# Perceiver block on one core: part of the probability transposes through DMAs, the second context through ScalarE, and a new order of the value products

## The chip, the cores and the metric

The kernel runs on 1 core of one Trainium2 chip. The metric is the device time of one execution in microseconds (us); before the change it is 512.61 us, the median of 3 runs (512.58 to 512.73).

## The reference, cut to what matters

`x` is two batches of 128 tokens by 512 features; the context is two batches of 2048 tokens by 512. The kernel computes three residual blocks; the change lies in the first.

```
k = split_heads(ctx @ Wk + bk); v = split_heads(ctx @ Wv + bv)   # 16 heads of 32
q = split_heads(layernorm(x) @ Wq + bq)
attn = softmax(q k^T / sqrt(32), over the 2048 context tokens)
x = x + (attn @ v) @ Wo + bo
x = x + self_attention(layernorm(x)) with its own layer norm, gamma, beta
x = x + FFN of 4 experts, one chosen per token (argmax), GELU, layer norm
```

All is float32. Products whose operands are split into a rounded part H and a rest L (type fp32r) are made as three matmuls (H*H, L*H, H*L).

## The kernel before, in words

The cross attention works in 8 steps `p` (NP = 8): batch `p // 4`, group `p % 4` of 4 heads (HPG = 4, G = 4). The 2048 context tokens lie in 4 chunks `c` of 512 (C = 4). There is no loop over steps that is shared by the engines: each engine has its own program, a queue that runs in order, and they meet at semaphores. In each program stands the loop `for p in range(1, NP + 1)` (L1502 TensorE, L571 ScalarE, L1032 VectorE); its turn `p` is called **pass p** here. Pass p makes the keys and the scores of step p, and turns the probabilities of step p-1 and multiplies them with the values.

What pass p holds, by function:

- `keys(p, c)`, TensorE (through `product`, L1158): 12 matmuls of 512 columns into PSUM bank 6 (bank 3 for c = 1). ScalarE then writes the rounded part `KrH` (L440), VectorE the rest `KrL` (L735). Both have KR = 3 slots, indexed by c.
- `scores(p, c)`, TensorE (L1212): 12 matmuls into banks 0 to 3, one bank per head, in three rounds of four heads. The first round of a chunk waits, head by head, until VectorE has read the chunk before (`s_done`).
- `negative_scores(p, c)`, VectorE (L755): per head, negates the scores into `Pm`, with the running minimum. It waits for the transpose of the same chunk and head of step p-1, which frees that place of `Pm`.
- `exponentials(p-1, i)`, ScalarE (L454): the exponential of head i over all 2048 tokens, in place in `Pm`.
- `probs_T(p-1, c, i)`: TensorE transposes four 128x128 blocks (L1228) of chunk c and head i into bank 4 or 5; ScalarE copies them into `PT` (L462), which has two slots (c % 2). I call one such unit a **turn**; a pass has 16.
- `weighted_values(p-1, c)`, TensorE (L1242): 32 matmuls with `V`, called WV(c) below. It ends the use of a slot of `PT` (`pv_mm`).
- `reciprocals_T` (L1250), `outputs`: the denominators. ScalarE copies the transposed reciprocals to `RT` (L470) between its second and third exponential.

The order of TensorE in pass p, written out by hand: keys 0, WV(3) of step p-2, `reciprocals_T`, keys 1, turns 0-0 and 0-1, keys 2, turns 0-2 and 0-3, scores 0, then for c = 1: two turns, WV(0), two turns, scores 1, keys 3; for c = 2: two turns, WV(1), two turns, scores 2; for c = 3: two turns, WV(2), two turns, scores 3. ScalarE: exp 0, KrH 0, exp 1, RT, exp 2, KrH 1, copies 0-0 and 0-1, exp 3, KrH 2, copies, and so on.

Some passes carry more. After pass 4 (p = G) come the 16 value products of batch 1 (`while_values`) with the self attention of batch 0 among them, which I call **the value stretch**. Passes 5 to 7 carry the rest of the self attention and the router of batch 0 (`alongside` on VectorE; `attention2_out` in pass 6; `normalized_T`, `logits` and `masks` in pass 7). Pass 8 has no keys and no scores, but the first expert matmuls (`first_experts`, L1423).

The context of batch 1 is loaded in passes 3 and 4: SyncE issues the four loads `raw` (L287) when the keys of pass 3 have read the chunk, and GpSimd makes `ctxH` (L400) and `ctxL` (L402) of each. GpSimd has nothing else to do in the passes, but for some `rsqrt` of one column (L385).

## Time and profile before

| | |
|---|---|
| median of 3 runs | 512.61 us |
| the profiled execution, its own time | 511.96 us |
| its span in the trace | 510.2 us |
| TensorE matmul busy | 494.2 us (97%) |
| VectorE busy | 304.8 us (60%) |
| ScalarE busy | 264.4 us (52%) |
| GpSimd busy | 42.2 us (8%) |
| TensorE clock granted | 9 or more tenths of full speed in all slices but the last (8 tenths) |

The profile is of one execution. Busy shares say little of where time can be won; the order of events within one pass says more, and this is read from the timeline (instructions of one engine in order) and from the chain that ended last. In those, "idle before" is the time that an engine stood still ahead of an instruction, with the instruction that released it.

### The profile page before, as it was taken

What the parts mean: (1) busy time and instruction counts of PE and PEld (TensorE: products, weight loads), DVE (VectorE), ACT (ScalarE), POOL (GpSimd) and SP (SyncE); (2) the same over time, 40 slices, a digit from 0 to 9 for tenths busy, and PEclk for the clock granted to TensorE, in tenths of its full rate; (3) what the DMA queues carried; (4) which work ended last, traced back from release to release, by engine and by line L of the source; (5) the groups of instructions that cost most, each with busy time, mean ns of one, the idle gap of its engine ahead of it and who ended that gap; (6) DMA issues with size and microseconds to landing.
All of it is one profiled execution on the core that took longest, in us unless ns stands there. A gap on an engine that the chain in (4) does not pass through costs nothing.

```text
span 510.2 us, 9250 instructions
## 1 busy us (share of the span) xinstructions
PE 494.2 (97%) x3742; PEld 377.6 (74%) x3742; DVE 304.8 (60%) x584; ACT 264.4 (52%) x400; POOL 42.2 (8%) x34
## 2 busy tenths in 40 slices
PE   8999998999999999999999999999999999999995
PEld 5786777777777777898877778766686867877663
DVE  3747542645565553246178376669379988965962
ACT  4230027485767632327347748567436756654730
POOL 0030000000099000000000000000002010000000
PEclk9999999999999999999999999999999999999998
DMA  8900000000341012220210000099377898875001
GB/s 279 360 1 1 1 1 0 2 1 1 94 162 79 1 45 109 96 84 0 82 65 3 0 1 1 10 418 397 107 284 294 302 387 362 297 288 240 1 0 41
DMA packets 11353, 62.47 MB, mean 122 GB/s; under 512 B 1584, under 2 KB 2096, under 8 KB 4528
## 3 DMA queue, kind: packets, MB, share of 16 engines
q1 hardware_dynamic: 11024, 61.62, 31.8%
q8 instruction: 30, 0.49, 0.4%
q10 hardware_dynamic: 288, 0.27, 0.2%
q14 instruction: 11, 0.09, 0.0%
HBM read 61.36 MB, written 0.52 MB: 121 GB/s over the span
## 4 chain that ended last, share of the span: by engine, by line
PE 84%; ACT 7%; issue 3%; DVE 2%; DMA 1%; SPq 0%; POOLq 0%; POOL 0%; ACTq 0%; DVEq 0%
PE ps L1158 36%; PE ps L1228 11%; PE ps L1242 6%; PE ps L1212 5%; ACT Pm L454 4%; PE ps L1479 3%; PE ps L1480 3%; PE ps L1481 3%; PE ps L1423 3%; PE ps L1499 3%; PE ps L1433 2%; PE ps L1435 2%; PE ps L1434 2%; DMA wv_raw<-in_xWv 1%; PE ps L1152 1%
## 5 line engine op out<-in xcount | busy, mean ns | idle before, releaser
L755 DVE TENSOR_SCALAR_CACHE_REDUCE Pm<-ps,small 128x512 f32<-128x512 f32 x96 | 66.4, 748 | 30.5 <-PE ps L1212 30.4
L462 ACT COPY PT<-ps 128x512 f32<-128x512 f32 x128 | 68.4, 591 | 29.0 <-PE ps L1228 29.0
L1228 PE MATMUL ps<-ident,Pm 128*128 128x128 f32 x512 | 69.3, 277 | 3.1 <-ACT Pm L454 3.1
L1228 PEld LDWEIGHTS ps<-ident,Pm 128*128 128x128 f32 x512 | 56.5, 141 | 18.0 <-issue 10.9
L454 ACT ACTIVATE Pm<-Pm,small 128x2048 f32<-128x2048 f32 x32 | 64.3, 2011 | 3.5 <-DVE Pm L755 3.5
L735 DVE SCALAR_TENSOR_TENSOR KrL<-ps,small,KrH 128x512 fp32r<-128x512 f32 x32 | 23.9, 747 | 61.2 <-ACT KrH L440 61.2
L1158 PE MATMUL ps<-wvH,ctxH 128*128 128x512 f32 x124 | 50.3, 406 | 1.0 <-DVE V L744 1.0
L1158 PE MATMUL ps<-ctxH,wkH 128*128 128x512 f32 x124 | 51.1, 412 | 0.0
L1158 PE MATMUL ps<-ctxL,wkH 128*128 128x512 f32 x124 | 48.6, 392 | 0.0
L1158 PE MATMUL ps<-ctxH,wkL 128*128 128x512 f32 x124 | 48.5, 391 | 0.0
L1158 PE MATMUL ps<-wvH,ctxL 128*128 128x512 f32 x124 | 48.4, 390 | 0.0
L1158 PE MATMUL ps<-wvL,ctxH 128*128 128x512 f32 x124 | 48.4, 390 | 0.0
L440 ACT ACTIVATE KrH<-ps,small 128x512 fp32r<-128x512 f32 x32 | 22.0, 688 | 47.2 <-PE ps L1158 46.6
L1124 DVE TENSOR_TENSOR w2L<-w2raw,w2H 128x2048 fp32r<-128x2048 f32 x15 | 34.2, 2289 | 10.7 <-ACT w2H L651 10.7
L651 ACT CAST w2H<-w2raw 128x2048 fp32r<-128x2048 f32 x15 | 28.7, 1911 | 19.0 <-PE ps L1481 18.5
L1242 PE MATMUL ps<-PT,V 128*32 128x128 f32 x1024 | 34.6, 276 | 1.0 <-ACT PT L462 1.0
L449 ACT COPY V<-ps 128x512 f32<-128x512 f32 x16 | 9.3, 584 | 47.8 <-PE ps L1158 45.3
L385 POOL TENSOR_TENSOR small<-small 128x1 f32<-128x1 f32 x10 | 6.8, 678 | 326.9 <-DVE small L716 326.9
L1242 PEld LDWEIGHTS ps<-PT,V 128*32 128x32 f32 x1024 | 26.0, 109 | 8.2 <-issue 6.0
L1158 PEld LDWEIGHTS ps<-ctxH,wkH 128*128 128x128 f32 x124 | 23.5, 190 | 9.3 <-issue 5.0
L1158 PEld LDWEIGHTS ps<-wvH,ctxH 128*128 128x128 f32 x124 | 23.3, 188 | 8.0 <-issue 2.0
L744 DVE COPY V<-ps 128x512 f32<-128x512 f32 x16 | 11.0, 689 | 29.3 <-PE ps L1158 29.3
(235 smaller groups left out, 869.9 us busy)
## 6 DMA issues: line engine op xcount, KB each, us to landing
w1raw<-in_W SPq DMA_DIRECT2D x16, 1024.0 KB, 6.1
w2raw<-in_W SPq DMA_DIRECT2D x15, 1024.0 KB, 4.9
raw<-in_ctxT SPq DMA_DIRECT2D x7, 1024.0 KB, 4.8
woF<-in_ffn_Wo SPq DMA_DIRECT2D x4, 1024.0 KB, 9.9
wo<-in_wo SPq DMA_DIRECT2D x2, 1024.0 KB, 4.9
ctx_first<-in_ctxT SPq DMA_DIRECT2D x4, 256.0 KB, 4.6
wv_raw<-in_xWv SPq DMA_DIRECT2D x2, 512.0 KB, 8.0
wq<-in_xWq SPq DMA_DIRECT2D x1, 1024.0 KB, 13.0
```

Source lines behind the costliest of these rows:

```text
L440: act.activation(KrH[:, c % KR, :], ps[:, bank, :], ACT.Identity, bias=bias3[:, 1, p % G:p % G + 1], scale=1.0).then_inc(k_hi, 1)
L454: act.activation(Pm[:, i, :], Pm[:, i, :], ACT.Exp, bias=mx[:, p % 2, i, C - 1:C], scale=-1.0, accum_out=den[:, p, i:i + 1]).then_inc(exp_ ...
L462: act.copy(PT[:, c % 2, i, :, :].rearrange("p k t -> p (k t)"), ps[:, t_bank(p, c, i), :]).then_inc(pt_done, 1)
L651: act.copy(w2H[n % 3][:], w2raw[n % RING2][:]).then_inc(w1_hi, 1)
L735: dve.scalar_tensor_tensor(KrL[:, c % KR, :], ps[:, bank, :], bias3[:, 1, p % G:p % G + 1], KrH[:, c % KR, :].bitcast(F32), ALU.add, ALU.s ...
L755: dve.tensor_scalar(Pm[:, i, c * CH:(c + 1) * CH], ps[:, i, :], -1.0, mx[:, p % 2, i, c - 1:c] if c else NOT_YET, ALU.mult, ALU.min, accum ...
L1124: dve.tensor_tensor(w2L[n % RING2][:], w2raw[n % RING2][:], w2H[n % 3][:].bitcast(F32), ALU.subtract).then_inc(w1_split, 1)
L1158: mm = pe.matmul(dst, l, r, start=(n == 0), stop=(n == len(pairs) - 1))
L1212: last = pe.matmul(ps[:, i, :], l[q, g, b * T:(b + 1) * T], r[q, c % KR, :], start=(k == 0), stop=(k == len(terms) - 1))
L1228: last = pe.transpose(ps[:, t_bank(p, c, i), j * P:(j + 1) * P], Pm[:, i, c * CH + j * P:c * CH + (j + 1) * P], ident[:])
L1242: last = pe.matmul(ps[q, PV_BANK, 0:T], V[:, c * JT + j, (HPG * g + i) * DH:(HPG * g + i + 1) * DH], PT[:, c % 2, i, j, :], start=(c == 0 ...
L1423: last = pe.matmul(ps[:, c, :], zt, w1raw[RAW_OF[t]][:, c * CH:(c + 1) * CH], start=(t == 0), stop=False)
```

## The change

1. For steps 0 to 6 (`by_dma`), heads 0 to 2 (HD = 3) of chunks 2 and 3 (PEC = 2) are no longer turned by TensorE. GpSimd copies the 512 words of each into `stage` as two planes of 512 half words (`probs_split`), SyncE issues a `dma_start_transpose` of 128 x 1024 half words (256 KB) from `stage` back into `Pm` (`turned`), and GpSimd weaves the planes together into `PT` (`probs_merged`). `stage` holds one head of each of the two chunks, so the copy of the next head waits for the DMA of the last. A turn remains for head 3 of these chunks: 10 of 16 turns in a pass stay with TensorE. Step 7 is turned as before.
2. `negative_scores(p, c)` of these heads waits for `merged[c]` instead of the transpose; WV(2) and WV(3) wait for `merged[c]` too.
3. KR is 2 instead of 3 (the room goes to `stage`): `KrH` of chunk c waits for the scores of chunk c-2. ScalarE makes it for chunk 2 behind the copies 0-2 and 0-3; VectorE makes `KrL` of chunks 2 and 3 behind the negations of chunks 0 and 1.
4. The loads of batch 1's context are issued by ScalarE, `ctxH` is made by ScalarE (`context_high`), `ctxL` by VectorE (`context_low`), in passes 3 and 4.
5. TensorE's order: WV(2) moves to the next pass, before WV(3); WV(0) and WV(1) stay among the turns and scores; keys 3 comes behind WV(1); the first 8 of the 12 matmuls of the next pass's keys 0 (EARLY) come before scores 3, but not in passes 3, 4 and 7 (`early_keys`). After pass 4, the first value product comes before WV(2) and WV(3).
6. The transposed outputs of batch 0's self attention (`outputs2_T`, pass 5) are all copied by ScalarE instead of half by VectorE. Some one-time semaphores are merged, and two `rsqrt` of GpSimd stand between its new copies.

The diff, cut to its core:

```diff
-        KR = 3
+        KR = 2
+        stage = at("stage", [P, 2, 2, CH], U16, 184)
...
+        def by_dma(p, c, i):
+            return p < NP - 1 and c >= PEC and i < HD
...
+        PEC = C // 2
+        HD = HPG - 1
...
@@ sync
-            for c in range(C):
-                sp.wait_ge(k_mm, C * (G - 1) + c + 1)
-                sp.dma_start(raw[c][:], a["ctxT"][C + c]).then_inc(raw_in[c], 16)
+            def turned(p, i):
+                for c in range(PEC, C):
+                    sp.wait_ge(p_split, 2 * (HD * p + i) + c - PEC + 1)
+                    sp.dma_start_transpose(Pm[:, i, c * CH:(c + 1) * CH].bitcast(U16).rearrange("p (k t) -> p k t", t=T),
+                                           stage[:, c - PEC, :, :].rearrange("p h n -> p (h n)")).then_inc(p_turned[c], 16)
...
@@ gpsimd
+            def probs_split(p, i):
+                pool.wait_ge(exp_done, HPG * p + i + 1)
+                for c in range(PEC, C):
+                    if HD * p + i:
+                        pool.wait_ge(p_turned[c], 16 * (HD * p + i))
+                    words = halves_of(Pm[:, i, c * CH:(c + 1) * CH])
+                    pool.tensor_copy(stage[:, c - PEC, :, :], words.rearrange("p n h -> p h n")).then_inc(p_split, 1)
+            def probs_merged(p, c, i):
+                pool.wait_ge(p_turned[c], 16 * (HD * p + i + 1))
+                if i == 0:
+                    pool.wait_ge(pv_mm, slot_user(p, c))
+                words = halves_of(PT[:, c % 2, i, :, :].rearrange("p k t -> p (k t)"))
+                halves = Pm[:, i, c * CH:(c + 1) * CH].bitcast(U16).rearrange("p (h n) -> p h n", h=2)
+                pool.tensor_copy(words.rearrange("p n h -> p h n"), halves).then_inc(merged[c], 1)
+            for p in range(NP - 1):
+                probs_split(p, 0)
+                probs_split(p, 1)
+                if p == G + 1:
+                    rsqrt(LN3[0])
+                probs_split(p, 2)
+                for i in range(HD):
+                    probs_merged(p, PEC, i)
+                if p == G + 1:
+                    rsqrt(LN4[0])
+                for i in range(HD):
+                    probs_merged(p, PEC + 1, i)
...
@@ scalar, keys(p, c)
-                    act.wait_ge(s_mm, (n if c == C - 1 else p * C) * HPG - (2 * HPG if c == C - 1 else 0))
+                    act.wait_ge(s_mm, (n - KR + 1) * HPG)
...
+            def context_in(c):
+                act.wait_ge(k_mm, C * (G - 1) + c + 1)
+                act.dma_start(raw[c][:], a["ctxT"][C + c]).then_inc(raw_in[c], 16)
+            def context_high(c):
+                act.wait_ge(raw_in[c], 32 if c else 16)
+                act.copy(ctxH[c][:], raw[c][:]).then_inc(ctx_hi1, 1)
...
@@ vector, negative_scores(p, c)
-                    if p:
-                        dve.wait_ge(t_mm, n - C * HPG + 1)
+                    if p and by_dma(p - 1, c, i):
+                        dve.wait_ge(merged[c], HD * (p - 1) + i + 1)
+                    elif p:
+                        dve.wait_ge(t_mm, turned_before(p - 1, c, i) + 1)
...
+            def context_low(c):
+                dve.wait_ge(ctx_hi1, c + 1)
+                dve.tensor_tensor(ctxL[c][:], raw[c][:], ctxH[c][:].bitcast(F32), ALU.subtract).then_inc(ctx_split1, 1)
...
@@ vector, the passes
                 for c in range(C):
                     if p < NP:
                         negative_scores(p, c)
-                        if c == 1:
-                            keys(p, 3)
+                        if p == G - 1 and c == 1:
+                            context_low(0)
+                        if c < 2:
+                            keys(p, c + 2)
+                        if p == G and c == 0:
+                            context_low(3)
+                        if p == G - 1 and c == 3:
+                            context_low(1)
...
@@ tensor, the passes
-                    keys(p, 0)
+                    keys(p, 0, (EARLY if early_keys(p) else 0, 3 * KT))
                 if late:
+                    weighted_values(p - 2, C - 2)
                     weighted_values(p - 2, C - 1)
                     reciprocals_T(p - 2)
...
+                    probs_T(p - 1, 1, 2)
+                    probs_T(p - 1, 1, 3)
+                    scores(p, 1)
+                    weighted_values(p - 1, 1)
+                    keys(p, 3)
+                    probs_T(p - 1, 2, 3)
+                    if p == G + 3:
                         masks(0)
+                    scores(p, 2)
+                    probs_T(p - 1, 3, 3)
+                    if early_keys(p + 1):
+                        keys(p + 1, 0, (0, EARLY))
+                    scores(p, 3)
                 if p == G:
+                    while_values(0)
+                    weighted_values(p - 1, C - 2)
                     weighted_values(p - 1, C - 1)
-                    while_values(0)
                     reciprocals_T(p - 1)
```

## Rows read from the trace of the kernel before

**Rows 1.** The page, part 1: busy us, share of the span, instructions.

```profile
PE 494.2 (97%) x3742; PEld 377.6 (74%) x3742; DVE 304.8 (60%) x584; ACT 264.4 (52%) x400; POOL 42.2 (8%) x34
```

**Rows 2.** The chain that ended last, 104 to 136 us: start, length, what.

```profile
104.16 2.96 PE ps L1158 x12
...
116.20 0.90 PE ps L1212 x11
117.10 1.02 PE ps L1228 x8
118.12 1.01 PE ps L1242 x32
...
121.06 2.95 PE ps L1158 x12
...
131.78 2.96 PE ps L1158 x12
```

**Rows 3.** Timeline of ScalarE, pass 3: start, length, instruction, idle before.

```profile
132.61 2.01 ACT L454 ACTIVATE Pm<-Pm,small 128x2048 f32<-128x2048 f32 x1 [0.59 <-DVE Pm L755]
...
135.34 2.00 ACT L454 ACTIVATE Pm<-Pm,small 128x2048 f32<-128x2048 f32 x1
...
140.99 2.03 ACT L454 ACTIVATE Pm<-Pm,small 128x2048 f32<-128x2048 f32 x1
```

**Rows 4.** Timeline of TensorE, pass 3: the turn that waits for the fourth exponential.

```profile
143.16 0.66 PE L1228 MATMUL ps<-ident,Pm 128*128 128x128 f32 x4 [0.36 <-ACT Pm L454]
```

**Rows 5.** Timeline of VectorE, end of pass 2 and pass 3.

```profile
127.84 0.75 DVE L755 TENSOR_SCALAR_CACHE_REDUCE Pm<-ps,small 128x512 f32<-128x512 f32 x1 [2.33 <-PE ps L1212]
...
130.53 0.18 DVE L764 RECIPROCAL small<-small 128x4 f32<-128x4 f32 x1
```

**Rows 6.** The page, part 5, and the groups by shape: GpSimd's and VectorE's context work.

```profile
L400 POOL CAST ctxH<-raw 128x2048 fp32r<-128x2048 f32 x4 | 7.6, 1900 | 108.6 <-DMA raw<-in_ctxT 108.6
L402 POOL TENSOR_TENSOR ctxL<-raw,ctxH 128x2048 fp32r<-128x2048 f32 x4 | 18.4, 4589 | 0.3
L728 DVE TENSOR_TENSOR ctxL<-raw,ctxH 128x2048 fp32r<-128x2048 f32 x3 | 6.9, 2291 | 0.1
```

**Rows 7.** DMA issues by line: count, KB each, median us from issue to landing.

```profile
rowsF<-in_rows SPq DMA_DIRECT2D x3, 256.0 KB, 8.6
b1raw<-in_b SPq DMA_DIRECT2D x1, 256.0 KB, 2.7
out_dram<-u SPq DMA_DIRECT2D x1, 256.0 KB, 2.0
```

**Rows 8.** Timeline of SyncE's queue: issue time of one DMA on an engine's queue.

```profile
188.45 0.33 SPq L290 DMA_DIRECT2D wS<-in_xWo  x1
```

**Rows 9.** The chain that ended last, at the borders of the other passes.

```profile
159.40 2.96 PE ps L1158 x12
...
252.95 5.67 PE ps L1158 x24
...
278.69 2.94 PE ps L1158 x12
...
309.21 2.95 PE ps L1158 x12
```

**Rows 10.** The same chain, passes 7 and 8.

```profile
329.84 0.70 ACT KrH L440
...
330.56 0.76 DVE KrL L735
...
339.92 3.67 PE ps L1423 x8
...
344.89 0.03 ACT RT L470
```

**Rows 11.** Timeline of VectorE, passes 5 and 6: the first instruction of each side job.

```profile
272.63 0.68 DVE L897 TENSOR_TENSOR u<-attnT,rows 128x512 f32<-128x512 f32 x1
...
296.98 0.75 DVE L908 SCALAR_TENSOR_TENSOR u<-u,small,rows 128x512 f32<-128x512 f32 x1
```

More of the change, by code:

```diff
@@ L13 @@
 F32R = mybir.dt.float32r
+U16 = mybir.dt.uint16
 ALU = mybir.AluOpType
@@ L240, in perceiver_block @@
         s_mm, s_done = sem("s_mm"), sem("s_done")
+        p_split = sem("p_split")
+        merged = {c: sem(f"merged{c}") for c in range(PEC, C)}
+        p_turned = {c: sem(f"p_turned{c}") for c in range(PEC, C)}
         exp_done, t_mm = sem("exp_done"), sem("t_mm")
@@ L314, in ffn_wo_in @@
                 sp.dma_start(woF[:, k, :], a["ffn_Wo"][:, k, :]).then_inc(woF_in, 16)
+            for p in range(G + 1, NP - 1):
+                for i in range(HD):
+                    turned(p, i)
             sp.wait_ge(k_mm, NP * C)
@@ L531, in values2, with outputs2_T @@
                 act.copy(V2[b][:].rearrange("p g d -> p (g d)"), ps[:, 4 * b, :]).then_inc(v2_ready, 1)
-            def outputs2_T(b):
+            def outputs2_T(b, heads):
                 act.wait_ge(cN_ready, b + 1)
-                for i in range(2, HPG):
+                for i in heads:
                     for a in range(HPG):
@@ L597, in _ @@
                             keys(p, 3)
-                        probs_T(p - 1, c, i)
+                            if p == G - 1:
+                                context_in(3)
+                        if not by_dma(p - 1, c, i):
+                            probs_T(p - 1, c, i)
                         if c == 3 and i == 1:
                             reciprocals(p - 1)
-                    if p == G + 1 and c == 1:
-                        outputs2_T(0)
+                    if p == G + 1 and c < 3:
+                        outputs2_T(0, range(2 * c - 2, 2 * c))
+                    if p == G - 1 and c < 3:
+                        context_high(c)
                 if p == G:
@@ L1159, in product, with keys @@
                 return mm
-            def keys(p, c):
+            def keys(p, c, part=(0, 3 * KT)):
                 b, g = divmod(p, G)
@@ L1174, in keys @@
                     pe.wait_ge(s_done, p * C * HPG)
-                product(ps[:, K2_BANK if p and c == 1 else K_BANK, :], [(w[:, k, f], t[:, k, :]) for k in range(KT)
-                                           for w, t in ((wkH, ctxH[c]), (wkL, ctxH[c]), (wkH, ctxL[c]))]).then_inc(k_mm, 1)
+                pairs = [(w[:, k, f], t[:, k, :]) for k in range(KT)
+                         for w, t in ((wkH, ctxH[c]), (wkL, ctxH[c]), (wkH, ctxL[c]))]
+                for n in range(*part):
+                    mm = pe.matmul(ps[:, K2_BANK if p and c == 1 else K_BANK, :], *pairs[n], start=(n == 0),
+                                   stop=(n == len(pairs) - 1))
+                if part[1] == len(pairs):
+                    mm.then_inc(k_mm, 1)
             def values(b, c, j):
@@ L1500, in ffn_out, with early_keys @@
                 last.then_inc(f_mm, 1)
+            EARLY = 8
+            def early_keys(p):
+                return 1 < p < NP and p not in (G, G + 1)
             for p in range(1, NP + 1):
@@ L1524, in _ @@
                     pe.wait_ge(v_dve, p // G * 2 * C + 2 * C)
[L1525 to L1541 removed]
+                if not more:
+                    for c in range(C):
+                        probs_T(p - 1, c, 0)
+                        probs_T(p - 1, c, 1)
+                        if c:
+                            weighted_values(p - 1, c - 1)
+                        else:
+                            first_experts(1)
+                        probs_T(p - 1, c, 2)
+                        probs_T(p - 1, c, 3)
+                else:
+                    probs_T(p - 1, 0, 0)
+                    probs_T(p - 1, 0, 1)
+                    keys(p, 2)
+                    probs_T(p - 1, 0, 2)
+                    probs_T(p - 1, 0, 3)
+                    scores(p, 0)
+                    probs_T(p - 1, 1, 0)
+                    probs_T(p - 1, 1, 1)
+                    weighted_values(p - 1, 0)
+                    probs_T(p - 1, 1, 2)
[5 more added lines that the diff above has]
+                    if p == G + 3:
+                        masks(0)
+                    scores(p, 2)
[3 more added lines that the diff above has]
+                    scores(p, 3)
                 if p == G:
+                    while_values(0)
+                    weighted_values(p - 1, C - 2)
                     weighted_values(p - 1, C - 1)
[L1544 removed]
                     reciprocals_T(p - 1)
```

122 lines of the change are left out of this document (62 added, 60 removed).

## Prediction

> **What bounds the kernel now.** The page says that TensorE is busy for 97% of the span [rows 1]. That tells only that nothing can be gained without taking work from it. What a removed matmul is worth is read from one steady pass, so the chain comes next [rows 2]: pass 2 runs from 104.16 to 131.78, 27.62 us. I count t from the start of a pass. The chain gives 1.02 for two turns (0.51 each), 1.01 for a WV, 0.90 for one chunk's scores, 2.95 for one chunk's keys [rows 2]. Then the other engines, to see how far each is from taking over. ScalarE starts its exponentials at t = 0.83, 3.56 and 9.21 (pass 3 starts at 131.78) [rows 2, 3], and TensorE's turn 0-3 already waits 0.36 us for the fourth, at t = 11.4 [rows 4]. So the first part of a pass, up to the end of scores 0 at t = 12.94 (at 117.10) [rows 2], is set by ScalarE as much as by TensorE. VectorE reads the four heads of a chunk in 2.7 us (127.84 to 130.53) [rows 5] and had waited 2.33 us before that: it is free in the second part, but not by much.
>
> **What the change removes.** 6 of 16 turns in 7 passes, 42 turns of 0.51 us: 21.4 us of TensorE. That would be the gain if TensorE set every moment. I go through a steady pass to see what takes over.
>
> *First part.* New order: the last 4 of 12 matmuls of keys 0 (0.98), WV(2) and WV(3) (2.02), the reciprocals, keys 1 (2.95), two turns, keys 2, one turn: some 10.4 us to turn 0-3, which can't start before t = 11.4, since the four exponentials, two KrH, RT and two copies on ScalarE stand as they were. The 1.97 us of keys 0 that were made early come back as a wait; WV(2) fits into it for nothing. Scores 0 end at 12.94 as before.
>
> *Second part.* Scores 1 end at 16.9 as before (at 121.06) [rows 2]. Then WV(1) to 17.9, keys 3 to 20.85. KrH 3 and KrL 3 follow (0.70 and 0.76) [rows 10], so VectorE is free at 22.35. The new order on VectorE puts KrL 3 ahead of the negations of chunk 2. These take 2.7 us, to 25.1. Scores 3 on TensorE must wait for them head by head: after turn 2-3, scores 2 (22.3), turn 3-3 (22.8) and the 8 early matmuls (24.7) TensorE waits 0.4 us for the last head, and ends near 25.8. A steady pass is 25.8 instead of 27.62: **1.8 us gained** where 3.1 us were removed; the rest stands as waits for ScalarE and VectorE. KR = 2 costs nothing here: KrH 2 waits for scores 0 (12.94), KrL 2 is done near 16.5, keys 3 want the bank at 17.9. Without early matmuls (passes 3, 4, 7) the wait for VectorE is longer by what they would have filled, and the end is the same.
>
> *The other passes*, each against its length before:
> - Pass 1: as a steady pass, -1.8. Pass 2: -1.8.
> - Pass 3 (131.78 to 159.40) [rows 2, 9]. ScalarE issues two loads among its exponentials (0.33 us each) [rows 8]: +0.7. A third load and a `ctxH` copy stand before the copies of turns 1-0 and 1-1. That copy is bounded by GpSimd's 1.90 us for the same tile [rows 6] from above; from below by half of it. I take 1.9. Turns 1-2 and 1-3 wait for those copies: +1.75. One `ctxL` (2.29) [rows 6] comes before KrL 3; most of it lies in VectorE's wait for KrH 3, and 0.45 shows. New length 25.8 + 2.9 = 28.7: **+1.1**.
> - Pass 4: keys 0 in full, the chain of two `ctxL` before keys 1 and 2, 0.9 in the first part; the `ctxH` copy costs 1.4 again. New length near 27.9: **+0.3**. Behind it WV(2) now stands in the open: 1.0, less the 0.3 that WV(3) no longer waits for its copies: **+0.7**. GpSimd's 6.5 us per chunk go, but nobody waited for them.
> - Pass 5 (252.95 to 278.69) [rows 9]: VectorE's two residual additions (from 272.63, 1.4 us) [rows 11] stand between KrL 3 and the negations of chunk 2, on the path now: gain only **-0.4**. The copies that go to ScalarE (8 more) fit in its idle time.
> - Pass 6 (278.69 to 309.21, 30.5) [rows 9]: here the first part is TensorE's (`attention2_out` stands in it), so early keys count, -0.9; the second part is VectorE's with its 1.5 us from 296.98 [rows 11] and statistics. **-1.5**.
> - Pass 7 (309.21 to 339.0, which is 339.92 less the wait of 0.9 that pass 8 begins with): first part -0.7, and `masks` wait for KrL 3 as before (KrH at 329.84, KrL at 330.56) [rows 10], with VectorE's negations behind them: 27.5 us against 29.8: **-2.4**.
> - Pass 8: WV(2) of step 6 stands before the reciprocals, whose copy RT at 344.89 [rows 10] is on the chain: **+1.0**.
>
> Sum: -1.8 -1.8 +1.1 +0.3 +0.7 -0.4 -1.5 -2.4 +1.0 = **-4.8 us**. The value stretch and all behind pass 8 stay.
>
> **What must be hidden for this.** Two new costs have no row: a GpSimd copy of 1024 half words (S) and a transposing DMA of 256 KB from issue to landing (L). For S, GpSimd's copy of 2048 words in 1.90 gives 0.95 for 1024 elements, its two-input subtraction 2.3 [rows 6]; I take 0.95, the nearer form. The two-byte strides could make it more, and I see no reason for less than 0.5. For L, 256 KB took 2.0 and 2.7 alone and 8.6 under load [rows 7]; the passes have nearly no other traffic, but small pieces may be slow. I take 3.5 and keep 2.0 to 8.6.
>
> With these: exponential 0 ends at 3.0, the three rounds (copy, DMA, next copy into the same `stage`) take 3 x (S+L) = 13.4, so chunk 2 is back at 16.4. Merges start at 15.0, behind WV(0), and head 2 of chunk 2 is merged near 18; VectorE wants it at 23.7. Chunk 3 is merged by 21, wanted at 25.8. The slack is used up when 3.0 + 3(S+L) + S = 23.7, so with S = 0.95 at S + L = 6.6, **L = 5.6**. GpSimd does 12 copies of 0.95, 11.4 us of 25.8.
>
> The Trainium skill (DMA: Bandwidth & Descriptors, section "Latency and other measured facts") gives 261 GB/s for a DMA transpose with a non-contiguous middle; by it the 256 KB would take 1.0 us behind a fixed cost, well inside the slack. No row here shows a transpose.
>
> **Rivals.**
> - *A. The transposing DMA is slow, slower than before.* Place: the three rounds through the one-head `stage`. Price: each us of L above 5.6 costs 3 us in each of passes 1 to 4, 6 and 7 (in pass 5 the work is long done), seen as VectorE waiting for `merged[2]`. It passes the old time from about L = 5.9. At L = 7 it is 3 x 1.4 x 6 = 25 us, so 533; at the upper row, 8.6, it is 54 us, so 562. For it: rounds can't overlap, and 2-byte pieces are unlike anything in [rows 7]. Against: 5.6 is twice the quiet row.
> - The Trainium skill (VectorE: DVE Perf Modes, section "The three transpose paths") gives 1309 ns for a 128x128 two-byte block by DMA; if the eight blocks of one DMA simply added up, L would be 10.5, an estimate from that page, and rival A would hold beyond its upper end, which I give 0.04 of A's chance. No row here bears on it.
> - *B. GpSimd's copies are slow.* With S = 2.3 a round takes S + L = 5.8, and the merges of chunk 2 end near 25.2 instead of 23.7: 1.5 us in 6 passes, 9 us, so about 517. For it: half-word strides; against: the copy row is at 0.93 ns per element.
> - *C. TensorE keeps more of the gain.* If VectorE's and ScalarE's waits in my pass are too large by 0.7 us each in 7 passes, 5 to 10 us more are gained: 498 to 503. Against: [rows 3, 4] show the wait for the exponential as there already.
> - *D. It does nothing*: the waits of passes 3 and 4 come out larger by 5 us, 512.6.
>
> **Numbers.** The profiled execution takes 511.96 (span 510.2), 0.65 less than the median of 512.61. From its own time: 511.96 - 4.8 = 507.2; against the median 512.61 - 4.8 = **507.8**, which I forecast. Chances: the forecast (504 to 511) 0.57; C 0.12; D 0.04; B and a mild A (513.6 to 520) 0.10; A above 520 0.17. The range that holds 8 in 10 leaves out most of A above and the far part of C: 501 to 520; the likeliest case alone spans 504 to 511. Faster by over 0.2% (below 511.6, about what a measurement can tell from no change): 0.70; within 0.2%: 0.05; slower: 0.25.
>
> **What would show it.** Transposes on TensorE x344 instead of x512, `PT` copies on ScalarE x86. Pass 2 near 25.8 us; turn 0-3 still waiting for the fourth exponential, with idle of 1 us or more instead of 0.36; VectorE's negations of chunk 2 right behind KrL 3. GpSimd near 11 to 12 us busy per pass, and its merges of chunk 2 starting when WV(0) ends, not when a DMA lands. If instead VectorE's idle before chunk 2 is released by GpSimd, or GpSimd stands waiting for a DMA after t = 20, A is true and L read from the issues says by how much. What would make the prediction wrong: L above 5.6, S above 2, or a GpSimd that slows VectorE while both work on SBUF; before, VectorE's negations took 0.75 us with GpSimd idle.

## The result, and the profile after

| | before | after |
|---|---|---|
| median | 512.38 us (511.51 to 512.85, 11 runs) | 513.7 us (512.76 to 517.68, 11 runs) |
| the profiled execution, its span | 511.96, 510.2 | 513.3, 511.4 |
| mean granted TensorE clock of a run, as a share of 2.4 GHz | 0.996 in the profiled execution, 0.995 to 0.999 in the runs beside the experiments | 0.976 to 0.988 |

The ratio is 1.004, with a 95% interval of 1.002 to 1.0059: a little slower, where 4.8 us less were forecast. The page of the kernel after (parts 1, 2 and 5; in part 5 "busy, mean ns" and then the idle time ahead of the group):

```profile
span 511.4 us, 8964 instructions
PE 487.0 (95%) x3574; PEld 366.5 (72%) x3574; DVE 317.2 (62%) x580; ACT 253.3 (50%) x370; POOL 120.3 (24%) x110
...
L437 POOL COPY stage<-Pm 128x1024 uint16<-128x1024 uint16 x42 | 45.4, 1097 | 137.1 <-ACT Pm L511 105.8
...
L446 POOL COPY PT<-Pm 128x1024 uint16<-128x1024 uint16 x42 | 58.8, 1471 | 33.7 <-PE ps L1339 33.3
...
L519 ACT COPY PT<-ps 128x512 f32<-128x512 f32 x86 | 46.9, 590 | 15.5 <-PE ps L1324 15.5
L1324 PE MATMUL ps<-ident,Pm 128*128 128x128 f32 x344 | 47.7, 277 | 6.3 <-ACT Pm L511 3.8
```

The edit did what it says: 344 transposes are left on TensorE and 86 copies on ScalarE. TensorE is busy for only 7.2 us less than in [rows 1], where 21.4 us of turns were removed. The DMAs that replace the turns, from issue to landing (the view of DMA issues: count, then us):

```profile
Pm<-stage SPq DMA_TRANSPOSE x42, 3.3
```

Where the time went shows pass by pass, from one pass border of the chain to the next, each against the same pass of before. A border is where scores 3 end; pass 5 starts with its keys and pass 8 with the first expert matmuls, so the wait of 0.9 us ahead of those counts to pass 7 in both kernels:

| | before | after | difference | forecast |
|---|---|---|---|---|
| start of pass 1 | 76.93 | 77.57 | +0.65 | 0 |
| pass 1 | 27.2 | 25.7 | -1.5 | -1.8 |
| pass 2 | 27.62 | 25.72 | -1.9 | -1.8 |
| pass 3 | 27.62 | 29.05 | +1.4 | +1.1 |
| pass 4 | 27.6 | 29.1 | +1.5 | +0.3 |
| value stretch | 65.95 | 66.62 | +0.7 | +0.7 |
| pass 5 | 25.74 | 25.97 | +0.2 | -0.4 |
| pass 6 | 30.5 | 30.7 | +0.2 | -1.5 |
| pass 7 | 30.7 | 28.4 | -2.3 | -2.4 |
| pass 8 | 21.6 | 23.9 | +2.3 | +1.0 |
| behind it | 148.7 | 148.6 | -0.1 | 0 |

The steady pass is right. Its border is seen in the chain of after (start, us, what), as [rows 2] has it for before:

```profile
114.30 0.66 PE ps L1324 x4
114.95 0.91 PE ps L1308 x11
...
125.74 1.85 PE ps L1269 x8
...
129.02 1.14 PE ps L1269 x4
```

Turn 0-3 starts at 114.30, 11.0 us behind the border at 103.28, and waits there for the exponential (0.88 us on TensorE's timeline, 0.36 in [rows 4]). The early keys run at 125.74. Pass 3 begins at 129.02.

Three places hold 4.2 of the 6.0 us that are missing in the table: passes 4, 6 and 8. In each of them the same work takes longer than in [rows 2] and [rows 10]. In the chain of after:

```profile
158.07 4.29 PE ps L1269 x12
...
281.28 3.12 PE ps L1339 x64
...
338.90 5.12 PE ps L1521 x8
344.02 1.89 PE ps L1339 x64
```

The twelve matmuls of keys 0 in pass 4 take 4.29 us instead of 2.96. WV(2) and WV(3), the same 64 matmuls, take 3.12 at 281.28 and 1.89 at 344.02. The first eight expert matmuls take 5.12 instead of 3.67. Together that is 4.0 us. The windows (stretch, length, busy us and count of PE, PEld, DVE, ACT and POOL, then the granted clock, the DMA share and GB/s) say why. Kernel after:

```profile
158.00:161.00 3.00, 3.00 (x8) 2.42 (x8) 2.96 (x9) 2.10 (x2) 1.41 (x2) 0.51 0.03 5
161.00:165.00 4.00, 4.00 (x74) 3.19 (x74) 3.68 (x3) 2.60 (x4) 3.68 (x2) 1.00 0.02 3
280.00:284.00 4.00, 4.00 (x60) 3.00 (x63) 3.13 (x9) 3.60 (x4) 1.44 (x2) 0.57 0.01 4
339.00:342.00 3.00, 3.00 (x4) 1.35 (x5) 3.00 (x9) 3.00 (x3) 0.00 (x0) 0.53 1.00 421
```

Kernel before, the same stretches of time:

```profile
158.00:161.00 3.00, 3.00 (x24) 2.16 (x23) 1.90 (x8) 2.04 (x4) 2.92 (x3) 1.00 0.02 5
280.00:284.00 4.00, 4.00 (x47) 3.03 (x46) 2.25 (x7) 3.95 (x4) 0.00 (x0) 1.00 0.01 2
339.00:342.00 3.00, 2.33 (x6) 1.10 (x7) 2.99 (x9) 2.41 (x4) 0.00 (x0) 1.00 1.02 429
```

The granted clock is 1.00 of 2.4 GHz before, and 0.51 to 0.57 after: for some 3 us the engine is at the 1.2 GHz level. It falls each time behind scores 3 of passes 3, 5 and 7. What TensorE did before that, on its timeline of after (start, us, what; in brackets the idle time ahead and who ended it):

```profile
152.14 0.66 PE L1324 MATMUL ps<-ident,Pm 128*128 128x128 f32 x4
154.37 0.47 PE L1308 MATMUL ps<-KrH,qH 32*128 32x512 f32 x1 [1.57 <-DVE Pm L838]
155.00 0.50 PE L1308 MATMUL ps<-KrH,qH 32*128 32x512 f32 x1 [0.17 <-DVE Pm L838]
156.24 0.49 PE L1308 MATMUL ps<-KrH,qH 32*128 32x512 f32 x1 [0.74 <-DVE Pm L838]
156.91 0.49 PE L1308 MATMUL ps<-KrH,qH 32*128 32x512 f32 x1 [0.18 <-DVE Pm L838]
```

These are the waits for VectorE's negations that the prediction has: scores 3 go out head by head, each behind a pause. Counted over all stretches of 2 us in which the clock is below 0.98, the last 5 us of the execution left out, 5.1 us of clock are missing in the profiled execution (0.64 granted over 2 us counts as 0.7 us). Before has no such stretch until 506 us, at its very end.

Not every such group of pauses is followed by a fall. In pass 4 of the same execution the pauses before scores 3 are 0.40, 0.17 and 0.18 us (at 184.29, 185.54 and 186.21), and the clock stays at 1.00.

The theory from here on: **the waits that the prediction left in place of the removed work cost more than they last, since TensorE's clock falls behind them, and the work that follows runs at half the clock.** Rivals: the chain of copies and DMAs sets the end of a pass somewhere (A or B of the prediction, in a mild form); the second context on ScalarE and VectorE costs the passes 3 and 4; the new order of TensorE loses what the turns gain.

### The profile page after: what moved, and what is told of

The parts are those of the page before. It is cut to its first block, busy times and chain, and to the rows that moved or that the text cites. A ratio compares the mean times of both kernels' runs of the same rounds, so it can differ in the third digit from the quotient of the medians.

```text
span 511.4 us, 8964 instructions
## 1 busy us (share of the span) xinstructions
PE 487.0 (95%) x3574; PEld 366.5 (72%) x3574; DVE 317.2 (62%) x580; ACT 253.3 (50%) x370; POOL 120.3 (24%) x110
## 4 chain that ended last, share of the span: by engine, by line
PE 78%; DVE 6%; issue 6%; ACT 5%; POOL 2%; DMA 1%; POOLq 0%; DVEq 0%; SPq 0%; ACTq 0%
PE ps L1249 23%; PE ps L1269 12%; PE ps L1324 5%; PE ps L1308 5%; PE ps L1339 5%; DVE Pm L838 3%; PE ps L1521 3%; PE ps L1577 3%; PE ps L1579 3%; PE ps L1578 3%; PE ps L1597 3%; ACT Pm L511 3%; PE ps L1531 2%; PE ps L1533 2%; PE ps L1532 2%
## 5 line engine op out<-in xcount | busy, mean ns | idle before, releaser
L437 POOL COPY stage<-Pm 128x1024 uint16<-128x1024 uint16 x42 | 45.4, 1097 | 137.1 <-ACT Pm L511 105.8
L446 POOL COPY PT<-Pm 128x1024 uint16<-128x1024 uint16 x42 | 58.8, 1471 | 33.7 <-PE ps L1339 33.3
L519 ACT COPY PT<-ps 128x512 f32<-128x512 f32 x86 | 46.9, 590 | 15.5 <-PE ps L1324 15.5
L1324 PE MATMUL ps<-ident,Pm 128*128 128x128 f32 x344 | 47.7, 277 | 6.3 <-ACT Pm L511 3.8
L1324 PEld LDWEIGHTS ps<-ident,Pm 128*128 128x128 f32 x344 | 38.4, 140 | 18.4 <-issue 10.8
L816 DVE SCALAR_TENSOR_TENSOR KrL<-ps,small,KrH 128x512 fp32r<-128x512 f32 x32 | 23.9, 746 | 43.9 <-ACT KrH L497 43.9
L1269 PE MATMUL ps<-ctxL,wkH 128*128 128x512 f32 x124 | 49.8, 401 | 0.0
L838 DVE TENSOR_SCALAR_CACHE_REDUCE Pm<-ps 128x512 f32<-128x512 f32 x32 | 20.2, 688 | 24.9 <-PE ps L1308 22.6
L1339 PEld LDWEIGHTS ps<-PT,V 128*32 128x32 f32 x1024 | 27.4, 113 | 8.7 <-issue 4.4
```

The costliest lines, as they stand in the source:

```text
L437: pool.tensor_copy(stage[:, c - PEC, :, :], words.rearrange("p n h -> p h n")).then_inc(p_split, 1)
L446: pool.tensor_copy(words.rearrange("p n h -> p h n"), halves).then_inc(merged[c], 1)
L519: act.copy(PT[:, c % 2, i, :, :].rearrange("p k t -> p (k t)"), ps[:, t_bank(p, c, i), :]).then_inc(pt_done, 1)
L838: dve.tensor_scalar(Pm[:, i, c * CH:(c + 1) * CH], ps[:, i, :], -1.0, mx[:, p % 2, i, c - 1:c] if c else NOT_YET, ALU.mult, ALU.min, accum ...
L1269: mm = pe.matmul(ps[:, K2_BANK if p and c == 1 else K_BANK, :], *pairs[n], start=(n == 0), stop=(n == len(pairs) - 1))
L1324: last = pe.transpose(ps[:, t_bank(p, c, i), j * P:(j + 1) * P], Pm[:, i, c * CH + j * P:c * CH + (j + 1) * P], ident[:])
```

## The experiments

The kernels e1 to e4 ran beside before at 512.44 us (25 runs), e5 to e8 beside 512.61 (8 runs), e9 and e10 beside 512.17 (7 runs). Ratios are to the kernel before of the same batch, with their 95% interval.

**Fill the wait (e1).** The kernel after, with transposes of the identity into a bank that nobody reads, at the place where TensorE waits:

```diff
+            def fill(p, n):
+                if n:
+                    pe.wait_ge(pt_done, turned_before(p - 1, 3, 3))
+                for k in range(n):
+                    pe.transpose(ps[:, t_bank(p - 1, 2, 3), (k % JT) * P:(k % JT + 1) * P], ident[:], ident[:])
...
+                    fill(p, {3: 16, 4: 16, 5: 8, 7: 16}.get(p, 0))
                     scores(p, 3)
```

> The changed kernel with idle TensorE time before scores 3 filled: 16 transposes of the identity (0.13 us each) into a free transpose bank in passes 3, 4 and 7, 8 in pass 5. Nothing else changes. Theory (clock): in the trace of the changed kernel the granted clock fell to 0.51 at 158 to 161 us, 0.57 at 280 to 284 and 0.53 at 339 to 342, each time behind the wait before scores 3, and the matmuls that follow took 4.29 instead of 2.95, 3.12 instead of 1.88 and 5.12 instead of 3.67 us: 4.0 us in all. With the waits filled the clock stays at 0.99 or more and the kernel takes 509.5 to 511, although it does 7 us more of TensorE work. Rival (plain waits): the time lost is the waits themselves, the added transposes at best fit into them: 513 to 515, with the clock where it was.

Measured: 510.18 us (508.62 to 512.86, 10 runs), ratio 0.9967 (0.9944 to 0.999). The time lies in the range expected. The kernel has 56 matmuls more than after and is 3.5 us faster. Its runs part by their mean clock: five of 508.62 to 509.87 us at 0.996 to 0.999, one of 510.5 at 0.993, four of 512.51 to 512.86 at 0.986 to 0.990. Its windows behind scores 3 of passes 3, 5 and 7:

```profile
158.00:161.00 3.00, 3.00 (x10) 2.33 (x10) 3.00 (x8) 2.09 (x2) 1.27 (x2) 0.64 0.00 0
...
280.00:284.00 4.00, 4.00 (x75) 3.24 (x74) 2.52 (x7) 4.00 (x4) 2.03 (x2) 1.00 0.00 0
...
339.00:342.00 3.00, 3.00 (x42) 1.58 (x44) 2.26 (x6) 2.36 (x4) 0.00 (x0) 1.00 1.02 426
```

The clock stays at 1.00 behind passes 5 and 7. Behind pass 3 it still falls: the filling takes up the first pause there, and pauses of 0.15, 0.75 and 0.17 us remain between the heads. What the clock alone costs is plain from pass 6 in e1's chain:

```profile
279.19 1.14 PE ps L1269 x4
...
308.31 1.14 PE ps L1269 x4
```

Pass 6 takes 29.1 us here, where after has 30.7 and 29.0 was forecast; pass 8 takes 22.5, where after has 23.9 and 22.6 was forecast. VectorE and GpSimd have the same work in both kernels. Pass 7, with its 16 transposes, is 0.7 us longer than in after. From e1's own runs the clock is worth about 3.6 us for each 0.01 of its mean (4.0 us between 0.997 and 0.986). By that, after at its median of 0.984 pays some 4.7 us against a run at 0.997: 513.7 - 4.7 = 509.0, an estimate, and it is where e1's runs at 0.996 to 0.999 lie.

**Without the second context (e2).** Its loads, splits and waits are left out, so the keys and values of batch 1 are made from the first context; this shows what part 4 of the change costs. The result is not the reference's.

```diff
             def context_in(c):
+                return
...
             def context_high(c):
+                return
...
             def context_low(c):
+                return
...
-                    pe.wait_ge(ctx_split1, c + 1)
```

> The changed kernel without the load and the split of the second context (passes 3 and 4): no context DMAs, no ctxH copies on ScalarE, no ctxL subtractions on VectorE; batch 1 is computed from batch 0's context, so this part of the computation is left out. Theory: passes 3 and 4 (29.0 and 29.1 us in the changed kernel) fall to the 25.7 of passes 1 and 2, 6.7 us in all, 1.35 of them from the clock: 506 to 508. Rival (the DMA and GpSimd chain is late in these passes for reasons of its own): they stay above 27.5 and the kernel above 510.

Measured: 509.77 us (506.58 to 512.95), ratio 0.9951 (0.9929 to 0.9972), above the 506 to 508 expected. Pass 3 is a steady pass of 25.72 us, where after has 29.05: the context costs pass 3 3.3 us, where the prediction had 2.9. Pass 4 is still 28.5, with the clock below full at 154 to 158 and 180 to 186. The runs have 0.978 to 0.992 of the clock. So the context is one part, but without it the clock still falls, at other places.

**Without the DMA turns (e3).** GpSimd's 84 copies and the 42 DMAs are left out; `PT` of these heads holds what was there. Nothing waits for `merged`, and GpSimd copies nothing beside VectorE. The result is not the reference's.

```diff
             for p in range(NP - 1):
-                probs_split(p, 0)
-                probs_split(p, 1)
...
-                    if p and by_dma(p - 1, c, i):
-                        dve.wait_ge(merged[c], HD * (p - 1) + i + 1)
+                        dve.wait_ge(exp_done, HPG * (p - 1) + i + 1)
```

> The changed kernel without the GpSimd copies and the transposing DMAs: heads 0 to 2 of chunks 2 and 3 are never turned and the value products read what PT held, so this part of the computation is left out. TensorE, ScalarE and VectorE keep their programs; VectorE waits for the exponential instead of the merge. Theory: the chain through the DMAs is hidden, so passes 1 and 2 stay at 25.7; what goes is the slowing of VectorE's subtractions beside GpSimd (3.28 and 3.03 instead of 2.29 us, small router steps 1.2 instead of 0.2): 1 to 3 us, 510.5 to 512.5. Rival A of the prediction (the three rounds are on the path): passes 1 and 2 shorten by over 1 us and the kernel falls below 507.

Measured: 513.27 us (509.07 to 514.41), ratio 0.9999 (0.997 to 1.0027). The expected 510.5 to 512.5 was missed: leaving the whole chain out makes the kernel no faster than after by more than its scatter, and the runs at 0.989 to 0.991 of the clock take 509.07 to 509.99, those at 0.981 513.73 to 514.41. In the profiled execution the clock also falls from 182 to 190 us, behind pass 4, where it doesn't in after. Passes 1 and 2 take 25.7 us each, as after: **the chain of copies and DMAs is hidden in a steady pass**, and rivals A and B fall there. In pass 3 it is not: that pass takes 27.25 us here and 29.05 in after. What e3 also changes is VectorE. The subtraction of its split takes 2.28 us at all three places, with GpSimd idle:

```profile
148.46 2.29 DVE L1060 TENSOR_TENSOR ctxL<-raw,ctxH 128x2048 fp32r<-128x2048 f32 x1
...
157.62 2.28 DVE L1060 TENSOR_TENSOR ctxL<-raw,ctxH 128x2048 fp32r<-128x2048 f32 x1
...
161.08 2.28 DVE L1060 TENSOR_TENSOR ctxL<-raw,ctxH 128x2048 fp32r<-128x2048 f32 x1
```

Kernel after, with GpSimd's merges (from 149.46) and splits (from 160.64) beside it:

```profile
149.62 3.28 DVE L1075 TENSOR_TENSOR ctxL<-raw,ctxH 128x2048 fp32r<-128x2048 f32 x1
152.82 0.74 DVE L816 SCALAR_TENSOR_TENSOR KrL<-ps,small,KrH 128x512 fp32r<-128x512 f32 x1
...
160.51 2.29 DVE L1075 TENSOR_TENSOR ctxL<-raw,ctxH 128x2048 fp32r<-128x2048 f32 x1
...
163.79 3.03 DVE L1075 TENSOR_TENSOR ctxL<-raw,ctxH 128x2048 fp32r<-128x2048 f32 x1
```

Two of the three subtractions, whose two inputs lie in SBUF, are 0.7 and 1.0 us longer; the instruction with one input in PSUM, beside the same copies, is not (0.74). The subtraction at 160.51 is not longer either. It started ahead of GpSimd's pair of splits (160.64), and there it is GpSimd that pays, on its own timeline of after:

```profile
110.52 2.16 POOL L437 COPY stage<-Pm 128x1024 uint16<-128x1024 uint16 x2 [2.43 <-DMA Pm<-stage]
...
160.64 4.04 POOL L437 COPY stage<-Pm 128x1024 uint16<-128x1024 uint16 x2 [1.59 <-ACT Pm L511]
```

The Trainium skill (SBUF — State Buffer, section "Who interferes with whom") says this of the pair: a VectorE instruction with two SBUF inputs contends with a GpSimd instruction that reads SBUF, and one with at most one SBUF input does not. The traces agree on both halves (2.29 to 3.28 us, and 0.75 to 0.74).

**The old order of TensorE (e4).** DMAs and the rest as after, but WV(1) and WV(2) among the turns as before, WV(3) alone in the next pass, and no early keys.

```diff
-                    weighted_values(p - 2, C - 2)
                     weighted_values(p - 2, C - 1)
...
-                return 1 < p < NP and p not in (G, G + 1)
+                return False
```

> The changed kernel with TensorE's order of before: keys 3 ahead of WV(1), WV(2) inside its own pass ahead of turn 3-3, no early keys, WV(3) before the first value product. Output as the reference's. Theory: the length of a steady pass is set by the exponentials in its first part and by VectorE's negations in its second, whatever TensorE does between: 25.6 to 25.8 us as in the changed kernel; the open WV(2) behind pass 4 and before pass 8's reciprocals go, -1 each; the wait before scores 3 gets longer, so clock drops may be more frequent: 510.5 to 513. Rival (the new order is what gives the 1.9 us of a steady pass): pass 2 back at 26.7 or more and the kernel at 518 or more.

Measured: 517.33 us (516.13 to 519.11), ratio 1.0102 (1.0077 to 1.0127). Missed: it was to be level with after. Pass 2 is 26.15 instead of 25.72, and passes 6 and 7 are 31.9 and 31.7 instead of 30.7 and 27.7 from scores 3 to scores 3. So the new order does not lose the gain; without it the kernel is 3.6 us slower, most of it in the passes that carry VectorE's work of batch 0. Its mean clock is 0.985 to 0.988, within the range of after.

**Each DMA twice (e5).** SyncE issues every transposing DMA a second time, behind the first, and GpSimd waits for both: the same result, twice the wait.

```diff
+                for again in range(2):
                     for c in range(PEC, C):
...
+                        if again:
+                            sp.wait_ge(p_turned[c], 32 * (HD * p + i) + 16)
...
```

> The changed kernel with each transposing DMA made twice, the second after the first has landed, so that L is about 6.6 us instead of the 3.3 measured. Theory (the sum of the prediction): the slack ends at L = 5.6 with GpSimd's copy at 0.95, and at 5.3 with the copies as measured (1.1 and 1.3 to 1.5 us); beyond it each us of L costs 3 us in each of six passes. So pass 2 grows from 25.7 to 29 to 31 us and VectorE's negations of chunk 2 wait for GpSimd: 530 to 545 in all. Rival (more slack than I think, the PT copies could start earlier and head 2 is wanted later): pass 2 stays under 27 and the kernel under 520.

Measured: 551.3 us (546.48 to 551.86), ratio 1.073 (1.0683 to 1.0776). Pass 2 takes about 30.0 us, as expected; passes 3 and 4 take 41.5 and 35, where the loads of the context lie beside. The mean clock is 0.948 to 0.961, and 24 us of it are missing in the profiled execution. Its DMAs (count, us to landing), and from the view of waits GpSimd's for them (us in total, times, longest):

```profile
Pm<-stage SPq DMA_TRANSPOSE x84, 3.2
```

```profile
POOL stage L440 <- DMA Pm<-stage: 82.5, 17, 10.0
```

With 6.4 us for a round trip the slack is used up and the price is there; at 3.3 it isn't. The total lies above the 530 to 545 expected. The new waits came with more clock missing (24 us for 5.1), and passes 3 and 4 grew by more than the sum has for them; how much of the excess is which was not separated.

**The context on VectorE (e6), and the side jobs (e7).** In e6 VectorE splits the context's chunks 0 and 3 in full, in its own idle time near the keys, so that ScalarE's `ctxH` is not ahead of the copies of turns 1-0 and 1-1, and pass 4's keys 0 start early. In e7 besides, VectorE's residual and statistics of passes 5 to 7 come before KrL 3, where it waits for ScalarE, and in pass 8 WV(2), WV(3) and the reciprocals come ahead of the first experts (the last three pieces of the diff).

```diff
-                return 1 < p < NP and p not in (G, G + 1)
+                return 1 < p < NP and p != G + 1
...
+                if p == G - 1:
+                    context_both(0)
+                if p == G:
+                    context_both(3)
...
+                        if c == 1:
+                            alongside(p, c)
                         if c < 2:
                             keys(p, c + 2)
...
-                    alongside(p, c)
+                    if c != 1:
+                        alongside(p, c)
...
+                if p == NP:
+                    first_experts(0)
```

> The changed kernel with chunks 0 and 3 of the second context split by VectorE alone, in its idle time ahead of scores 0 of passes 3 and 4, and so with early keys in pass 3 too. Output as the reference's. Theory: ScalarE's ctxH copies no longer stand ahead of the copies of turns 1-0 and 1-1 (1.26 us of wait in pass 3 and in pass 4), no subtraction stands ahead of KrL 3 in pass 3, and the wait of 4 us before scores 3 of pass 3 with the clock drop behind it (1.35 us) goes: pass 3 from 29.0 to about 26, pass 4 from 29.1 to 26.5; 513.7 less 5 to 6 is 508 to 509. Rival (VectorE is full: what it takes on comes back elsewhere): no more than 2 us gained.

> e6_context_vector with VectorE's residual (pass 5) and statistics (pass 6) moved ahead of KrL 3, where it waited 1.96 us for KrH 3, and with WV(2), WV(3) and the reciprocals ahead of the first expert matmuls in pass 8. Output as the reference's. Theory: pass 5 loses 1.4 to 1.6 us, pass 6 about 1, pass 8 about 2 (RT is on the chain there), and the clock drop behind pass 5 goes in some executions: 503 to 506. Rival (the chain of pass 8 is set by the exponentials, and passes 5 and 6 by GpSimd's slowing of VectorE): 507 or more.

Measured: e6 509.68 us (507.61 to 511.11), ratio 0.9934 (0.9908 to 0.9959), with pass 3 at 26.8 and pass 4 at 27.7 instead of 29.05 and 29.1. That is 4.0 us less than after, and 0.7 to 1.7 above the expectation. e7 507.71 us (507.23 to 508.73), ratio 0.9903 (0.9888 to 0.9918). Its expectation of 503 to 506 was missed, and the time is the one that its rival had (507 or more). Its clock is still 0.986 to 0.989: it no longer falls behind pass 5, but it does behind pass 4 (180 to 188 us) and behind pass 7 (334 to 340).

**All of it (e8).** e7 with transposes of the identity before scores 3, 4 in passes 3 and 5, 16 in passes 4 and 7.

```diff
+                    fill(p, {3: 4, 4: 16, 5: 4, 7: 16}.get(p, 0))
                     scores(p, 3)
```

> e7_side_jobs with filled waits before scores 3: 4 transposes of the identity in passes 3 and 5, 16 in passes 4 and 7. Output as the reference's. Theory (clock): the drop left behind pass 7, and any behind pass 4, goes, 1.4 to 2.5 us less than e7_side_jobs: 501 to 504, with a granted clock of 0.995 or more. Rival (plain waits): no faster than e7_side_jobs.

Measured: 504.96 us (504.41 to 506.51), ratio 0.9851 (0.9828 to 0.9874), clock 0.994 to 0.999. The step from e7 is a little more than expected, the time itself 1 us above the range. **This version beats both kernels, by 1.5% against before.** Only 40 matmuls of no use set it apart from e7, and they make it 2.7 us faster. Pass 8 in its chain:

```profile
332.45 1.89 PE ps L1345 x64
...
334.59 3.44 PE ps L1527 x8
```

WV(2) and WV(3) take 1.89 and the experts 3.44, where after has 5.12.

**No early keys (e9), and the same with filling (e10).** The sharpest test of the step that failed. The prediction says of passes without early matmuls that the wait is longer and "the end is the same".

```diff
-                return 1 < p < NP and p not in (G, G + 1)
+                return False
```

e10 has this edit and 16 filling transposes in each of passes 1 to 7.

> The changed kernel without early keys: all 12 matmuls of keys 0 stand at the start of every pass, so TensorE's wait before scores 3 is longer by up to 1.97 us in passes 1, 2, 5 and 6, as it is in passes 3, 4 and 7 already. The prediction's way of counting (a wait is worth what it lasts, and a pass ends where VectorE ends) gives nothing for the longer wait itself; only the first part of passes 2, 3, 6 and 7 grows by 0.7 to 1.0 us, since WV(2), WV(3) and the whole of keys 0 stand ahead of turn 0-3: 513.7 + 3.4 = about 517, with pass 1 as before. The clock theory adds a stretch at the 1.2 GHz level behind the new waits of passes 1, 2, 5 and 6, of about 1.3 us each, as measured in passes 3, 4 and 7: about 522, with pass 1 near 27 instead of 25.7 and more stretches of granted clock under full.

> As e9_no_early, with 16 transposes of the identity, which nobody reads, before scores 3 in passes 1 to 7; they lie in the wait where it is long enough (2.0 us at full clock). Plain counting: the same time as e9_no_early, or slower by what the transposes stick out of the wait (up to 1 us a pass). Clock theory: faster than e9_no_early by 5 to 9 us, near 514, with a granted clock of 1.00 right behind every scores 3 and pass 1 back near 25.8.

Measured: e9 528.44 us (523.25 to 529.72), ratio 1.0297 (1.0242 to 1.0351), clock 0.962 to 0.972. e10 516.99 us (515.48 to 517.81), ratio 1.0082 (1.0059 to 1.0106), clock 0.991 to 0.995. **112 matmuls that compute nothing make the kernel 11.4 us faster.** Plain counting allowed no gain at all; the clock theory gave 5 to 9 us, and it was more. e9 itself was expected near 517 by plain counting and near 522 with the clock, and is slower than both; e10, with most of the clock back, lands on the 517 of plain counting. e4 fits in: it has no early keys either, but WV(2) stands before its scores 3, and it takes 517.33 us at 0.985 to 0.988. In the profiled execution of e9 17.1 us of clock are missing, in that of e10 3.4. TensorE around scores 3 of pass 2 in e9:

```profile
126.06 1.08 PE L1308 MATMUL ps<-KrH,qH 32*128 32x512 f32 x2 [0.40 <-DVE Pm L838]
127.31 1.46 PE L1308 MATMUL ps<-KrH,qH 32*128 32x512 f32 x2 [0.18 <-DVE Pm L838]
...
129.56 0.80 PE L1269 MATMUL ps<-ctxH,wkH 128*128 128x512 f32 x1
130.15 0.63 PE L1269 MATMUL ps<-ctxH,wkL 128*128 128x512 f32 x1
```

and in e10:

```profile
127.58 1.91 PE L1611 MATMUL ps<-ident 128*128 128x128 f32 x16
129.42 1.14 PE L1308 MATMUL ps<-KrH,qH 32*128 32x512 f32 x4
...
130.95 0.50 PE L1269 MATMUL ps<-ctxH,wkH 128*128 128x512 f32 x1
131.29 0.40 PE L1269 MATMUL ps<-ctxH,wkL 128*128 128x512 f32 x1
```

A matmul of 512 columns takes 0.63 in the one and 0.40 in the other. The windows of e9 and e10 for the same stretch, in this order:

```profile
126.00:134.00 8.00, 7.58 (x23) 4.86 (x24) 4.79 (x15) 2.88 (x4) 1.80 (x2) 0.60 0.01 3
```

```profile
126.00:134.00 8.00, 7.86 (x63) 5.63 (x65) 6.29 (x18) 3.91 (x6) 1.96 (x3) 1.00 0.01 3
```

Two points of the expectations were missed. In pass 1 of e9 the same waits (0.40, 0.17 and 0.17 us) stand before scores 3, and the clock stayed at 1.00. In e10 it should have been 1.00 behind every scores 3, and pass 1 near 25.8 us; it still fell behind pass 3 (160 to 166 us), where pauses of 0.56, 0.68, 0.73 and 0.18 us remain, and inside pass 1 (90 to 94 us), which takes 27.3. Ahead of that fall stands a wait of 1.50 us for the fourth exponential, and after has the same wait at the same place with the clock at 1.00 behind it. What makes the clock fall behind one wait and not behind another is not told by these runs.

## Why the prediction was wrong

It forecast 507.8 us, and 513.7 came. 5.9 us are missing; the table of passes adds up to 6.0 in the profiled executions.

**The step that failed** is the one under "Second part": the waits before scores 3 were named, placed and sized, and then priced at what they last ("the wait for VectorE is longer by what they would have filled, and the end is the same"). What the runs showed in its place: TensorE's clock can fall behind these waits, and the matmuls that follow then take 1.3 to 1.7 times as long, 4.4 us more in all in the profiled execution. By its own steps:

- *The steady pass*: right. 25.8 forecast, 25.72 and 25.7 measured; turn 0-3 waits 0.88 us for the fourth exponential (1 us or more was named); the negations of chunk 2 stand right behind KrL 3; merges start when WV(0) ends (118.06).
- *S and L*: L 3.3 for 3.5; S 1.10 for the split and 1.47 for the merge for 0.95. S + L is 4.4 to 4.8 against a bound of 6.6. e3 and e5 show from both sides that this is hidden, so A and B had the right place and the right sign of their condition. The two estimates that the prediction took from the Trainium skill are 1.0 us and a fixed cost by the rate (DMA: Bandwidth & Descriptors, section "Latency and other measured facts") and 10.5 us by the block time (VectorE: DVE Perf Modes, section "The three transpose paths"); the 3.3 measured lies between. Rival B's sum doesn't come out of its terms: with S = 2.3, 3.0 + 3 x 5.8 + 2.3 is 22.7 and not 25.2, and by GpSimd's queue, with two copies in each round, it is about 26. Nothing hangs on it, since S came out well below 2.3.
- *Pass 3*: +1.4 for +1.1, and it is by luck that these lie so near. The prediction had 2.9 us for ScalarE's and VectorE's work on the context and nothing for the DMA chain. With that work and without the chain (e3) the pass takes 27.25 us, 1.5 above a steady pass. The other 1.8 come with the chain: `ctxL` took 3.28 us beside GpSimd for the 2.29 of [rows 6], and rounds of the DMA beside the loads of the context took long. The 0.7 for the issues of the loads didn't come at all: turn 0-3 starts 11.0 us behind the border (at 140.02), as in pass 2. In the chain of after:

```profile
134.53 6.42 DMA Pm<-stage
...
149.46 3.22 POOL PT L446 x2
...
154.00 2.18 POOL PT L446 x2
```

  Here, in this one pass, the chain of DMAs does reach the end of the pass. It is rival A in a mild form, at most 1.8 us large, the slowed `ctxL` included.
- *Pass 4*: +1.5 for +0.3. **This is the first place of the failing step.** Keys 0 take 4.29 us for 2.96, and these 1.3 us are all that is missing.
- *Value stretch*: +0.7, right.
- *Pass 5*: +0.2 for -0.4. The residual addition `u` takes 0.96 us beside GpSimd for 0.68 before, and without GpSimd's copies (e3) the pass takes 25.7 instead of 26.0: that is 0.3 of the 0.6. The other 0.3 stays open.
- *Pass 6*: +0.2 for -1.5. The clock takes nearly all of it: WV(2) and WV(3) take 3.12 us for 1.89, and the four matmuls of keys 0 ahead of them 1.48 for 1.13, 1.6 us together. With the clock at 1.00 (e1) the pass takes 29.1 us, 0.1 above the forecast. VectorE's addition `x_sb`, two inputs in SBUF, was slowed beside GpSimd's copies:

```profile
300.35 1.66 DVE L993 SCALAR_TENSOR_TENSOR x_sb<-u,small,x_sb 128x512 f32<-128x512 f32 x1
```

  It costs the pass nothing: it takes 1.67 us in e1 and 0.75 in e3, without the copies, and pass 6 takes 29.1 in both.
- *Pass 7*: -2.3 for -2.4, right.
- *Pass 8*: +2.3 for +1.0. The experts' 5.12 us for 3.67 are 1.45, all that is missing.
- *Start*: +0.65, before the first pass. e1, e4, e9 and e10 have the same work there and start pass 1 between 76.83 and 77.37 us: it is scatter of executions for the most part.

So 4.4 us of the 6.0 lie in three stretches behind such waits, 0.65 at the start, and about 1 us in passes 1, 3 and 5. "The rest stands as waits for ScalarE and VectorE" was taken to mean that they cost no more than the work that they replace. That work kept TensorE at 2.4 GHz; a wait in its place doesn't always. The Trainium skill (TensorE: Matmul & The Clock Gate, section "A second HAM failure mode: psum-queue depth-cycling") tells of another kernel in which short pauses between groups of matmuls made the clock swing between its two levels. The traces here agree as far as they go: behind pauses of 0.17 to 1.57 us the clock was 0.51 to 0.57. The profile before showed no fall ahead of its last slice. In it, scores 3 of passes 3, 5 and 7 stand behind the last turn with no pause; that this is the reason was argued, not tested by itself. The prediction named "a GpSimd that slows VectorE" among what would make it wrong; that came, as a smaller term. None of its rivals held the clock.

**Shown:** that filling the waits brings the time back (e1, e7 to e8, e9 to e10), that the DMA chain is hidden in a steady pass (e3, e5), that the chain does reach the end of pass 3 (e3), that VectorE's instructions with two inputs in SBUF and GpSimd's copies slow each other (e3). **Argued only:** why the kernel before had no falls. **Open:** 0.3 us of pass 5; when exactly the clock falls; runs of one and the same kernel differ in it (after 0.976 to 0.988, e1 0.986 to 0.999).

## What to carry to other kernels

Work taken from a TensorE that was always busy doesn't turn into time where another engine is close behind it; it turns into waits. In this kernel such a wait could cost more than it lasted, because the matmuls behind it ran at half the clock. So price a new wait with the granted clock behind it in mind, fill it with work that was due anyway (early keys) or with matmuls of no use, and look at the granted clock by stretch before looking for a mechanism elsewhere. When work goes to GpSimd, look at which instructions of VectorE beside it read two operands from SBUF.

## What the runs showed of the hardware

- Pauses before scores 3 of 1.57, 0.17, 0.74 and 0.18 us were followed by some 3 us at 0.51; in e9 pauses of 0.40 and 0.18 us were followed by some 8 us with 0.60 granted. In pass 4 of after and in pass 1 of e9 pauses of 0.40 and twice 0.17 to 0.18 us were followed by none. The 16 transposes ahead of scores 3 in e10, with 1.00 granted behind them in pass 2, take 1.91 us.
- A transposing DMA of 128 x 1024 half words within SBUF takes 3.3 us from issue to landing (the median of 42), and its issue 0.66 us in the chain (SPq at 133.82); in pass 3, beside loads of 1 MB, the chain waits 6.42 for one.
- GpSimd copies 1024 half words per partition in 1.10 us when the read is strided and 1.47 when the write is, in the mean. Beside VectorE's `ctxL` one of the two pays: where `ctxL` started first (160.51), it took 2.29 and GpSimd's pair of splits 4.04 instead of 2.16; where it started second (149.62, 163.79), it took 3.28 and 3.03.
